# Moving the second normalization, the transposes and the router of a decoder layer from a stage of their own into the cross attention, batch by batch

## The reference, cut to what matters

```
x = layernorm(x + self_attention(x))            # 16 heads of 8, causal
x = layernorm(x + cross_attention(ctx, x, mask)) # 16 heads of 64, keys: 512 context rows and 256 tokens
x = layernorm(x + experts(x))

def experts(x):
    probs = softmax(x @ w_router)               # 8 experts
    top 2 of them, gates = their probs over their sum
    y_e = (silu(x @ w1[e]) * (x @ w3[e])) @ w2[e]      # hidden 256, every expert on every token
    return sum_e gate_e * y_e + (silu(x @ sw1) * (x @ sw3)) @ sw2
```

## Time and profile before

| | before |
|---|---|
| time, median of 3 runs | 1175.52 us (1174.66 to 1175.65) |
| profiled execution: its time, its span | 1176.83 us, 1175.0 us |
| PE busy | 1116.9 us, 95% of the span |
| DVE, ACT, POOL busy | 882.1, 740.0, 509.4 us |
| mean granted clock of PE | 0.985 |

### The profile page before, as it was taken

How to read it: one execution, slowest core, us unless ns; L and a number is a source line. 1 busy time by engine, 2 the same in 40 slices (tenths; PEclk the granted TensorE clock), 3 DMA queues, 4 the chain that set the end, 5 groups by cost and what they waited for, 6 DMA issues and landing times. The chain is left out here.

```text
span 1175.0 us, 27356 instructions
## 1 busy us (share of the span) xinstructions
PE 1116.9 (95%) x8781; PEld 959.5 (82%) x8781; DVE 882.1 (75%) x2763; ACT 740.0 (63%) x1756; POOL 509.4 (43%) x790
## 2 busy tenths in 40 slices
PE   6999997999999999999999999999999986999997
PEld 5887875788888888887888888888888766999997
DVE  7999996887787878787877778787877756555554
ACT  6999995676566667666756657666766644222221
POOL 4666674554454554364445545455433324000101
PEclk9999999999999999999999999999999996899999
DMA  2000013000000000000000000000000000000000
GB/s 90 7 7 11 7 43 107 25 11 1 2 10 1 2 1 11 2 2 10 2 1 11 1 2 1 1 2 1 1 2 1 2 1 1 1 10 6 9 8 9
DMA packets 14649, 12.36 MB, mean 11 GB/s; under 512 B 1328, under 2 KB 13616, under 8 KB 14384
## 3 DMA queue, kind: packets, MB, share of 16 engines
q1 hardware_dynamic: 14096, 10.43, 2.8%
q10 hardware_dynamic: 416, 0.20, 0.1%
HBM read 9.57 MB, written 1.05 MB: 9 GB/s over the span
## 5 line engine op out<-in xcount | busy, mean ns | idle before, releaser
L852 POOL TENSOR_TENSOR xk_parts<-k_raw,xk_parts 64x768 fp32r<-64x768 f32 x128 | 236.6, 1848 | 341.4 <-DVE xk_parts L964 339.2
L988 DVE CUSTOM_DVE_ANT_0 xmasked<-ps,bar 128x768 f32<-128x768 f32 x256 | 244.3, 954 | 4.6 <-issue 0.7
L1073 PE MATMUL ps<-xk_parts,xq_parts 128*128 128x512 f32 (+1 forms) x1024 | 233.6, 350 | 6.5 <-DVE xq_parts L969 3.4
L901 ACT ACTIVATE xprobs<-xmasked,xlow 128x768 f32<-128x768 f32 x256 | 238.0, 930 | 1.0 <-DVE xlow L988 1.0
L1079 PE MATMUL ps<-ident,xprobs 128*128 128x128 f32 x1536 | 215.1, 276 | 5.8 <-DVE xlow L988 4.6
L1073 PEld LDWEIGHTS ps<-xk_parts,xq_parts 128*128 128x128 f32 x1024 | 174.2, 189 | 33.4 <-DVE xlow L988 5.5
L1079 PEld LDWEIGHTS ps<-ident,xprobs 128*128 128x128 f32 x1536 | 169.2, 141 | 15.2 <-DVE xlow L988 8.9
L1090 PE MATMUL ps<-xprobs_t,xvals 128*64 128x256 f32 x1536 | 179.9, 383 | 1.1 <-ACT xprobs_t L907 1.1
L1090 PEld LDWEIGHTS ps<-xprobs_t,xvals 128*64 128x64 f32 x1536 | 104.9, 137 | 57.7 <-issue 10.5
L993 DVE COPY xprobs_t<-ps 128x768 f32<-128x768 f32 x128 | 121.6, 950 | 4.5 <-PE ps L1079 4.5
L1267 ACT ACTIVATE xvals<-ps 128x512 f32<-128x512 f32 x72 | 42.8, 597 | 123.2 <-PE ps L1380 123.2
(11 more groups left out here) (212 smaller groups left out, 2468.4 us busy)
## 6 DMA issues: line engine op xcount, KB each, us to landing
ctx_in<-in_ctx SPq DMA_DIRECT2D x8, 256.0 KB, 3.5
w_up<-in_L_ffn_w SPq DMA_DIRECT2D x2, 1024.0 KB, 6.8
raw_kv<-in_L_xattn_Wkv SPq DMA_DIRECT2D x1, 1024.0 KB, 5.3
out<-state SPq DMA_DIRECT2D x8, 128.0 KB, 2.0
x_in<-in_x SPq DMA_DIRECT2D x7, 128.0 KB, 2.1
raw_q<-in_L_xattn_Wq SPq DMA_DIRECT2D x1, 512.0 KB, 6.1
wout<-in_L_xattn_Wout SPq DMA_DIRECT2D x1, 512.0 KB, 3.7
keep_all<-in_mask_BxS_bk SPq DMA_DIRECT2D x1, 512.0 KB, 4.9
```

The lines of the kernel that those rows point to most:

```text
L852: pool.tensor_tensor(k_parts[dst, i // 2 % 2, h, :], k_raw[src, :], k_parts[src, i // 2 % 2, h, :].bitcast(F32), ALU.subtract).then_inc(k_ ...
L901: nc.scalar.activation(probs[:, i % 4, :], masked[:, i % 4, :], ACT.Exp, scale=-1.0, bias=low[:, i % 4:i % 4 + 1], accum_out=sums[:, pair ...
L988: dve.tensor_tensor_reduce(masked[:, i % 4, :], slot(slots.place("S", i), KEYS), bar[:, par, :], 1.0, 3e38, ALU.add, ALU.min, low[:, i % 4 ...
L1073: last = nc.tensor.matmul(slot(s, hi - lo, lo), q_parts[:, pair % 2, h, part, t * P:(t + 1) * P], k_parts[:, pair % 2, h, lo:hi], start=pa ...
```

## The change

1. The blocks of `normalize` and `experts` are gone. There is one block, and each engine goes on from the list of the cross attention to that of the experts.
2. The second normalization is done per batch in the round after it. POOL gets five steps `N3` (places 8 to 12, between those of `N2`), DVE `NORM2` (place 15).
3. The transposes of `state` go into PE's step `TX` of two batches later (same slot, second bank), the router's matmuls into `TC` of two batches later. ACT copies the transposed tokens in its step `TX`, DVE has `XHI` (place 19, rounding) and `LOGITS` (place 20, copy), POOL `XLO` (place 21, low part). There is now a `TX` and a `TC` for a ninth batch, for the sake of batch 6. Batch 7 has these steps between those of the first batch of the experts.
4. The next user of the slot of `TX` waits for ACT's second copy, that of the slot of `TC` for DVE's `LOGITS`.
5. The choice of the best two is done for batches 0 to 6 in the last round of the cross attention (12 steps at places 20.5 to 26, the exponential on ACT at 27, 6 steps from 28.5) and for batch 7 in the experts (12 steps after `Y` of expert 6 of the first batch, the exponential in the second batch).
6. Weights of the first three experts are loaded where all were loaded before, and split in round 1 of the cross attention. The weights of the other six, and `w_down`, are loaded when the last `PT` is done, into memory that the cross attention has left. ACT rounds them behind the first two `silu`; POOL makes two low parts, then `N3` of batch 7, then the other four.
7. PE does `H` of experts 0 and 1 of the first batch in front of the last `OUT`.

```diff
+        last = B - 1
+        ahead = [("H", 0, i) for i in range(r.AHEAD)]
...
-                c.pool_order.run(emit, done=("N1", "N2", "Y"))
+                c.pool_order.run(emit, {1: steps(more, "UP", r.FIRST, 3, 2)}, done=("N1", "N2", "Y"),
+                                 left=[("N3", last), ("XLO", last)])
+                for at in range(r.FIRST, r.FIRST + 2):
+                    more("UP", 0, 0, at)
+                for at in range(5):
+                    emit("N3", last, last % 2, at)
+                for at in range(r.FIRST + 2, NE):
+                    more("UP", 0, 0, at)
+                more("XLO", last, last % 2, 0)
+                e.tail_order.run(more)
...
+                c.act_order.run(emit, {1: steps(more, "UP", r.FIRST, 2, 2), last: steps(more, "EXP", 1, 27, 1), B: steps(more, "H", r.AHEAD, 5, 1)},
+                                done=("TX", "TC"))
+                for at in range(r.FIRST, NE):
+                    more("UP", 0, 0, at)
...
+                c.dve_order.run(emit, {last: steps(more, "ROUTE", r.BEFORE_EXP, 20.5, 0.5)
+                                      + [(28.5 + 0.3 * n, lambda n=r.BEFORE_EXP + n: more("ROUTE", 0, 0, n))
+                                         for n in range(r.STEPS - r.BEFORE_EXP)],
+                                       B: steps(more, "H", r.AHEAD, 5.5, 0.25)},
+                                done=("STATS", "NORM1", "NORMED", "BAR", "Y"), left=[("NORM2", last), ("XHI", last), ("LOGITS", last)])
+                e.dve_order.run(more, left=ahead, between={0: [(4.25, lambda: emit("NORM2", last, last % 2, 0)),
+                                           (7.25, lambda: more("XHI", last, last % 2, 0)),
+                                           (8.25, lambda: more("LOGITS", last, last % 2, 0))]
+                                       + [(8.4 + 0.04 * n, lambda n=n: more("ROUTE", 1, 0, n)) for n in range(r.BEFORE_EXP)],
...
+                c.pe_order.run(emit, {B: steps(more, "H", r.AHEAD, 2, 1)}, done=("TX", "TC"))
+                e.order.run(more, left=ahead, between={0: [(6.5, lambda: more("XT", last, last % 2, 0)), (8, lambda: more("LOGITS", last, last % 2, 0))]})
...
-        normalize(nc, sem, "n2", B * T, state, stats, mean, rstd, var, tmp)
...
+            if kind == "TX" and b >= 2:
+                act.wait_ge(full["TX"], b + 1)
+                wait(act, r.x_ready, b - 3)
+                wait(act, r.logits_out, b - 3)
+                nc.scalar.activation(r.xt[:, par, :], slot(slots.place("TX", 0), S, BANK), ACT.Copy
+                                     ).then_inc(r.xt_copied, 1)
...
+            if kind == "TX" and b >= 2:
+                pe.wait_ge(r.renormed, b - 1)
+                for j in range(T):
+                    last = nc.tensor.transpose(slot(s, P, BANK + j * P), state[:, (b - 2) * T + j, :], ident[:, :])
+            if kind == "TC" and b >= 2:
+                pe.wait_ge(r.xt_copied, b - 1)
+                for j in range(T):
+                    last = nc.tensor.matmul(slot(s, E, BANK + j * E), r.xt[:, par, j * P:(j + 1) * P], m.w_rt[:, :],
+                                            start=True, stop=True)
...
+            if kind == "NORM2":
+                dve.wait_ge(r.scaled, b + 1)
+                for j in range(T):
+                    tokens = state[:, b * T + j, :]
+                    last = dve.tensor_scalar(tokens, tokens, r.moments[4][:, j:j + 1], r.moments[5][:, j:j + 1],
+                                             ALU.subtract, ALU.mult)
+                last.then_inc(r.renormed, 1)
...
+    def loads(sp):
+        sp.wait_ge(*c.transposed)
+        for n, routed in enumerate((m.w1, m.w3)):
+            sp.dma_start(w_rest[:, n, :, :], routed[FIRST - 1:E].rearrange("e d h -> d e h")).then_inc(m.loaded_rest_up, 16)
+        sp.dma_start(w_down[:, 0, :, :], m.sw2.rearrange("(k p) d -> p k d", p=P)).then_inc(m.loaded_down, 16)
+        sp.dma_start(w_down[:, 1:NE, :, :].rearrange("p e k d -> p (e k) d"),
+                     m.w2.rearrange("e (k p) d -> p (e k) d", p=P)).then_inc(m.loaded_down, 16)
```

More of the change, by code:

```diff
@@ L46, with __init__ @@
 class Order:
[L53 to L54 removed]
+    def __init__(self, batches, units, starts, beyond=()):
+        self.batches, self.beyond = batches, beyond
         due = []
@@ L63, in __init__, with has, run @@
         assert all(-1 <= rel <= 1 for _, rel, _ in self.steps)
-    def run(self, emit, between=None, done=()):
+    def has(self, kind, batch):
+        return 0 <= batch < self.batches + (kind in self.beyond)
+    def run(self, emit, between=None, done=(), left=()):
         between = between or {}
@@ L73, in run @@
                     inserted.pop(0)[1]()
-                if 0 <= w + rel < self.batches and not (w == -1 and kind in done):
-                    emit(kind, w + rel, (w + rel) % 2, i)
+                b = w + rel
+                if self.has(kind, b) and not (w == -1 and kind in done) and (kind, b) not in left and (kind, b, i) not in left:
+                    emit(kind, b, b % 2, i)
             for _, insert in inserted:
@@ L100, in before @@
             batch = batch + (rel2 - rel - (n < self.places))
-            if not isinstance(batch, int) or 0 <= batch < self.batches:
+            if self.order.has(kind, batch):
                 return kind, batch, i
@@ L237, in _ @@
             @block.tensor
             def _(pe):
-                emit = c.tensor(pe)
+                emit, more = c.tensor(pe), e.tensor(pe)
                 a.tensor(pe, {B: steps(emit, "TX", 1, 4, 1) + steps(emit, "TC", 1, 4, 1)})
-                c.pe_order.run(emit, done=("TX", "TC"))
-        x_mem.close()
-        normalize(nc, sem, "n2", B * T, state, stats, mean, rstd, var, tmp)
[L245 to L298, removed]
@@ L798, in finished, with chain @@
             return semaphore, batch * per + i + 1
-        def chain(b, group, tiles, link, scaled):
-            gap, total, var, fix, mean, root = (moments[n][:, tiles] for n in range(6))
-            me, ve, mo, vo = (early.stats[:, tiles, i] for i in (1, 2, 4, 5))
-            half, three = (early.powers[:, n, 0:tiles.stop - tiles.start] for n in range(2))
+        def chain(b, group, measures, results, link, scaled):
+            gap, total, var, fix, mean, root = results
+            me, ve, mo, vo = (measures[:, :, i] for i in (1, 2, 4, 5))
+            half, three = (early.powers[:, n, 0:measures.shape[1]] for n in range(2))
@@ new lines, in cross_attention, with last_user, experts @@
+    c.transposed, c.summed, c.done = (full["PT"], B * UNITS), (pv_done, B * PAIRS), (added, B)
+    c.heads_ready = heads_ready, B * PAIRS
+    def last_user(s):
+        uses = [(B - 1 + (k in pe_order.beyond), rel, at, k, i) for at, (k, rel, i) in enumerate(slots.mine)
+                if slots.place(k, i) == s]
+        b, _, _, kind, i = max(uses, key=lambda u: (u[0] - u[1], u[2]))
+        return taken(kind, b, i)
+    c.last_user = last_user
+    return c
+def experts(nc, sem, sb, ps, slot, m, r, c, mem):
+    B, S, D, T, E, NE, HID, HB = m.B, m.S, m.D, m.T, m.E, m.NE, m.HID, m.HB
+    ident, state, FIRST = m.ident, m.state, r.FIRST
+    logits, index, best, first, chosen, scratch, gap, gate, gates = (
+        r.logits, r.index, r.best, r.first, r.chosen, r.scratch, r.gap, r.gate, r.gates)
```

519 lines of the change are left out of this document (296 added, 223 removed).

## The result

The changed kernel takes **1154.36 us** (median of 4, 1154.3 to 1154.66) where the kernel before takes 1175.1 (4 runs): a ratio of 0.9824, 95% interval 0.9807 to 0.9841, about 20.7 us less. The forecast was 1158.0. The profiled execution has a span of 1152.5 us in place of 1175.0, 22.5 less; the forecast had 17.5 less for both. (The profiled execution of the kernel before took 1176.83, more than its median; that of the changed kernel took its median.)

What follows compares the result with a forecast made beforehand. PE, busy 95% of the span, was taken as the bound, idle or half-clocked only at the switch. 27.4 - 6.3 - 2.0 - 0.65 - 1.0 = 17.5 us saved gave a median of 1158.0, range 1152 to 1168 for 8 in 10.

Steps and rivals of the forecast that it cites:

- The switch, 27.4 us: Between last `OUT` and `Y` of expert 2: 36.34 us less 8.98 of needed PE work, all 27.4 us gained.
- The step about the slot: At the switch: first `H` takes the slot of `R`, free when ACT's copy ends at 967.24, and runs from 967.3.
- What made up those 27.4 us: At the switch: idle 8.1, transposes 3.65, router 6.8, then `H` and `Y` at half clock with the first `Y`'s wait.
- The added steps, 0.9 us a batch, 6.3 in all: Cross attention, seven batches: 0.65 PE transposes and router, 0.15 stall from ACT's second copy, 0.10 DVE; bounds 4.6 to 19.8.
- The choice in the last round, 2.0 us: DVE's 12 steps at places 20.5 to 26, lengthened beside about three POOL key steps; PE loses 2.0, between 0 and 7.9.
- 5 us worse than mine: Estimate by the port-lock rule: the choice takes 9 us, with a whole POOL key step at three meetings; exposed, sum 5 worse.
- The experts, 1.65 us lost: Expert stage: 0.65 for `XT` and router of batch 7 on PE, 1.0 for choice, exponential and `NORM2` (between 0 and 4).
- Stronger disturbance of the cross attention: Rival: added steps cost 2.5 us a batch in the cross attention in place of 0.9, giving 1169; chance 0.15.
- Late weights: Rival at the switch: loads need twice the time, `Y` of expert 0 waits some 7 us, giving 1165; chance 0.09.
- `NORM2` waiting for `N3`: Slower rival, cross attention: late `N3` on POOL stops DVE and the masks in seven batches; at 5 us late, 1182; chance 0.05.
- The clock: Rival at the switch: small gaps keep the clock low, five `H`, two `Y` and `OUT` cost 12.8 us, giving 1171; chance 0.05.
- The signs named: Profile after: `OUT`s 96.5 us apart, no PE idle over 1.5, `Y` every 2.33, last round longer by at most 5.

Runs made afterwards that it cites:

- e10: Changed kernel with the loads of the later weights started when the last `PV` is done instead of the last `PT`, 3.8 us later; 1157.57 us.
- e8: Kernel before, with 56 transposes of the identity on PE into an unread PSUM bank during the second normalization; 1175.93 us, ratio 1.0003.
- e1: Changed kernel with the router's two matmuls of each step `TC` done twice; 1156.84 us.
- e2: Changed kernel with DVE's rounding copy `XHI` done three times in each batch of the cross attention; 1155.35 us.
- e3: Changed kernel without the choice of the best two for batches 0 to 6, their gates set to 0.25 by one memset; 1154.53 us.
- e4: Changed kernel with the rounded weights of experts 3 to 8 moved by 448 bytes, equal to the tokens' address modulo 512; 1156.84 us.
- e5: Changed kernel with 64 unused bytes before the weights of experts 0 to 2, putting these at 64 and experts 3 to 8 at 128 modulo 512; 1155.30 us.
- e9: Changed kernel with 64 unused bytes before the weights of experts 0 to 2 and 448 before those of 3 to 8, both at 64 modulo 512; 1152.70 us.

## Why the prediction was right, step by step

- *The switch, 27.4 us.* Right: 27.97. The step about the slot was wrong by 0.65 us: `H` of expert 0 does not have the slot of `R`, since turns are also counted for steps of batches that do not exist, and it began when `R` ended. The wait for the slot of `OUT` was as stated (0.52). Loads, roundings and `N3` were in time; `w_down` by 0.6 us, at the lower end of the stated 0.5 to 3 (e10).
- *What made up those 27.4 us.* Here the text set the clock beside the waits. e8 does not part the two: where the clock was kept up, the chain through DVE and POOL took its place, and from the first `Y` on some 2.5 us of low clock stayed. The total did not depend on it, because it was taken from first to last and not as a sum of its parts.
- *The added steps, 0.9 us a batch, 6.3 in all.* The size was right: 0.94 a batch. Of PE's own 0.65, the router's 0.43 cost its full length (e1); the transposes were not doubled. The rest is 0.29, where 0.25 was taken, but it is not made up as stated, and that its size fits is luck. The text had 0.15 for `K` behind ACT's second copy, which was 0.05 (0.32 for 0.27), and 0.10 for DVE's steps. What it did not have is the wait of 0.23 for the raw keys, which comes from `N3` ahead of `LO` on POOL. And DVE's steps are less well hidden than it said: of what e2 adds, a third shows.
- *The choice in the last round, 2.0 us.* Mis-sized: 0.4 (e3). The step that failed is the one from the total of the operations to the loss. DVE's idle stretches took them up, and of the three meetings with POOL that were counted in, one happened. On what the text drew from the Trainium skill ("SBUF — State Buffer"): that rule would have cost up to 9 us only with POOL's operations beside the steps; the trace agrees with it in the one step that began in a `LO`, 0.44 us long in place of 0.27. The text's "5 us worse than mine" does not follow from its terms, which are 9 and 2.0 and so 7 apart.
- *The experts, 1.65 us lost.* 1.33 gained. The pace gives 45 x 0.05 = 2.3 us or somewhat more; without it (e4) this part is 168.22 - 167.17 = 1.05 us longer than before, where 1.65 was forecast. No row of the kernel before could show this term, since all of its weights lay at the same place modulo 512.
- *The sum.* 17.5 forecast and 22.5 measured: 0.6 from the switch, 1.5 from the cross attention (the choice 1.6), 3.0 from the experts. Without the term of the pace, which nobody foresaw, the kernel takes 1156.84 (e4), 1.2 from the forecast of 1158.0.
- *The rivals.* Stronger disturbance of the cross attention: no (0.94 a batch, and the last round 1.46). Late weights: no, but by 0.6 us only. `NORM2` waiting for `N3`: no; POOL ended `N3` of a middle batch at 438.79, and DVE took it up at 441.55. But `LO` waited behind `N3`, on the same engine. The clock: 1.00 throughout.
- *The signs named.* Distance of the additions 96.5, longest wait of PE at the switch 1.10 us, last round 1.46 longer: as stated. `Y` at 2.33: it was 2.27. Router steps near 1.2 us in the last round: the longest was 0.44.

## What to carry to other kernels

Work that sits between two stages bound by one engine costs the whole time from the last step of the one to the even pace of the next, less what that engine has to do there anyway. Moved into the stages, it costs what it puts on that engine, nearly in full. What it puts on another engine can be hidden for the most part (here two thirds on DVE, idle a fifth of the time), but since the lists are run in order, it also delays what stands behind it: look at what each added step is put in front of. A low clock seen in a stretch isn't yet its whole cause: ask which engine's chain would remain if it were high, and what that chain would then meet. When a change also moves tiles, compare the pace of untouched matmuls on both sides before giving the difference to the order of work.

## What the runs showed of the hardware

- The pace of the same matmul (128x128 weights in the rounded type, 256 columns, clock 1.00) changes when weights are moved within a partition: 114.5 to 119.1 ns from start to start, by shifts of 64 and 448 bytes. The addresses of its own two operands do not fix it (e5 and e9, experts 1 and 2: 117.3 and 114.5).
- In e8 the clock fell from 1.00 to 0.50 (0.85 from 982 to 985) while PE was recorded busy 3.00 of 3 us. What it did there were the router's matmuls, 32 pieces of 8 columns; ahead of them it had been idle for 0.49 and 0.24 us.
- A rounding of 128x1024 on DVE took 0.69 and 0.71 us with POOL idle for most of it, and 1.58 and 1.77 beside POOL's low parts (before and e8).
